# Attention and pair products in one kernel: six of eight key steps on kept score pieces instead of five

## The reference, cut to what matters

```
# layer 0: attention over the 4096 positions of one image
xf   = gn(x)                                   # (4, 256, 4096)
f, g = Wq xf + bq,  Wk xf + bk                 # 32 channels each
h    = Wv xf + bv                              # 256 channels
s    = einsum('bki,bkj->bij', f, g)            # 4096 x 4096 scores per image
beta = softmax(s, axis=1)                      # over i
x    = x + gamma * einsum('bci,bij->bcj', h, beta)
# layer 1: products of all channel pairs
y    = relu(bn(w1 gn(x) + b1))                 # 32 channels
packed = y[rows] * y[cols]                     # 528 pairs
x    = x + relu(bn(w2 packed + b2))
```

## Time and profile before

| what | value |
|---|---|
| median of three runs | 2107.17 us |
| profiled execution, its own time | 2109.38 us |
| its span (first to last instruction) | 2107.6 us |
| TensorE matmuls busy | 2056.0 us (98%) |
| VectorE busy | 1656.5 us (79%) |
| ScalarE busy | 1539.2 us (73%) |
| GpSimd busy | 1479.8 us (70%) |
| DMA queue q1, share of 16 engines | 66.6% |
| chain that ended last, share of TensorE | 86% |

### The profile page before, as it was taken

One profiled execution on the slowest core, in us unless ns is written; L12 is line 12 of the kernel. 1 busy time (PEld: TensorE's weight loads), 2 busy tenths in 40 slices (PEclk: granted clock), 3 DMA queues, 4 the chain that ended last, 5 costly groups with the idle time before them and its releaser, 6 DMA issues.

```text
span 2107.6 us, 48084 instructions
## 1 busy us (share of the span) xinstructions
PE 2056.0 (98%) x17334; PEld 1611.1 (76%) x17334; DVE 1656.5 (79%) x3617; ACT 1539.2 (73%) x2456; POOL 1479.8 (70%) x2110
## 2 busy tenths in 40 slices
PE   5899999999999999999999999999999999999999
PEld 3688888888877777777877777777787777777854
DVE  8788988778777877878768788777877768777767
ACT  5677777767776777778777787777777777777767
POOL 3265666667677777878768787777867767677766
PEclk9999999999999999999999999999999999999999
DMA  5165778776476788778478678887836767675632
GB/s 190 37 101 103 129 143 143 139 132 113 84 133 122 146 158 150 154 145 156 98 140 140 117 156 142 159 167 139 157 78 134 144 124 140 118 142 94 139 72 81
DMA packets 728269, 271.89 MB, mean 129 GB/s; under 512 B 674240, under 2 KB 681152, under 8 KB 728000
## 3 DMA queue, kind: packets, MB, share of 16 engines
q1 hardware_dynamic: 728032, 268.82, 66.6%
HBM read 77.07 MB, written 19.92 MB: 46 GB/s over the span
## 4 chain that ended last, share of the span: by engine, by line
PE 86%; DVE 5%; POOL 3%; ACT 2%; issue 2%; DMA 1%; SPq 0%; DVEq 0%; ACTq 0%; POOLq 0%
PE acc L1784 19%; PE acc L1772 19%; PE acc L1773 18%; PE tps L1577 5%; PE acc L1577 5%; PE sps L1597 4%; PE acc L1571 3%; PE tps L1648 3%; PE tps L1650 2%; PE acc L1648 1%; POOL kb L1162 1%; PE tps L1612 1%; DVE ks L863 1%; PE tps L1634 1%; POOL xl L1139 1%
## 5 line engine op out<-in xcount | busy, mean ns | idle before, releaser
L1162 POOL TENSOR_TENSOR kb<-ks,kb 128x512 f16<-128x512 f32 x630 | 760.3, 1211 | 412.1 <-DVE kb L891 315.6
L1772 PE MATMUL acc<-hth,kt 128*128 128x257 f16 x2520 | 587.2, 273 | 1.1 <-DMA kt<-kb 1.1
L1773 PE MATMUL acc<-htl,kt 128*128 128x256 f16 x2520 | 586.6, 273 | 0.0
L1333 ACT ACTIVATE ph<-sps,esc 128x512 f16<-128x512 f32 x394 | 269.5, 684 | 339.7 <-PE sps L1597 329.8
L1345 ACT ACTIVATE ks<-ks,kbias,esc 128x512 f32<-128x512 f32 x630 | 498.9, 805 | 0.0
L1784 PE MATMUL acc<-hth,kt 128*128 128x257 f16 x2520 | 385.8, 274 | 0.0
L863 DVE TENSOR_SCALAR_CACHE_REDUCE ks<-acc 128x512 f32<-128x512 f32 x378 | 259.2, 686 | 158.8 <-PE acc L1577 157.0
L1772 PE MATMUL acc<-hth,ph 128*128 128x257 f16 x1576 | 367.3, 274 | 0.0
L1773 PE MATMUL acc<-htl,ph 128*128 128x256 f16 x1576 | 366.9, 273 | 0.0
L1784 PEld LDWEIGHTS acc<-hth,kt 128*128 128x128 f16 x2520 | 247.7, 98 | 100.6
L1772 PEld LDWEIGHTS acc<-hth,kt 128*128 128x128 f16 x2520 | 247.0, 98 | 41.6 <-issue 6.2
(11 more groups left out here) (254 smaller groups left out, 3444.7 us busy)
## 6 DMA issues: line engine op xcount, KB each, us to landing
rt<-turned SPq DMA_DIRECT2D x96, 256.0 KB, 4.9
xt<-x SPq DMA_DIRECT2D x46, 512.0 KB, 4.5
xb<-x SPq DMA_DIRECT2D x32, 512.0 KB, 4.7
out<-zt SPq DMA_DIRECT2D x45, 256.0 KB, 2.7
kt<-kb SPq DMA_TRANSPOSE x630, 3.2
yb<-turned SPq DMA_DIRECT2D x36, 128.0 KB, 2.6
rt<-turned SPq DMA_DIRECT2D x72, 64.0 KB, 2.2
turned<-yb SPq DMA_DIRECT2D x12, 256.0 KB, 2.5
```

The source lines that it names most:

```text
L1162: tt(kb[:, m % KB_RING, 1], ks[:, m % KS_RING], kb[:, m % KB_RING, 0], ALU.subtract).then_inc(kl_ok, 1)
L1333: A(ph[:, v % SLOTS], sps[v % 2][:], ACT.Exp, scale=esc[:]).then_inc(ph_ok, 1)
L1772: mm(bank[:, 0:C + 1], high[:, q], hth[:, c * QT + q], start=(s8 == 0 and q == 0), stop=False)
L1773: mm(bank[:, 0:C], high[:, q], htl[:, c * QT + q], start=False, stop=False)
```

## The change

`KEPT_STEPS` grows from five to six (1, 2, 3, 5, 6, 7), so steps 0 and 4 alone are made. The sixth kept number (r = 5) has its low half made by VectorE right after its cast (`LOW_BY_DVE`), counted by a semaphore of its own, `kd_ok`; GpSimd keeps five low halves per tile. ScalarE makes three high halves per tile in place of two, VectorE still makes three casts. The tables of steps are set anew, and the rings `ks`, `kb` and `kt` get one slot more each. For that memory the ring of x falls from 14 to 13 chunks. So one chunk more per image passes through `xt`, and `VORD` and `V_EARLY` are changed.

```
-KEPT_STEPS = (1, 2, 4, 6, 7)
+KEPT_STEPS = (1, 2, 3, 5, 6, 7)
-HIGH_BY_ACT = (0, 2)
-EXP_AT = (3, 4, 6, 7, 8)
-CAST_AT = (None, 3, None, 6, 7)
-LOW_AT = (2, 3, 5, 7, 8)
-TURN_AT = (3, 4, 6, 8, 9)
+HIGH_BY_ACT = (0, 2, 4)
+EXP_AT = (1, 2, 4, 5, 6, 8)
+CAST_AT = (None, 1, None, 4, None, 7)
+LOW_AT = (0, 2, 3, 5, 6, None)
+TURN_AT = (2, 3, 5, 6, 7, 9)
+LOW_BY_DVE = (5,)
-ROW_AT = 6
+ROW_AT = 5
-KS_RING = 8
-KB_RING = 4
-KT_RING = 5
+KS_RING = 9
+KB_RING = 5
+KT_RING = 6
-XR = 14
+XR = 13
...
-        VORD = (4, 0, 5, 1, 6, 2, 3, 7)
+        VORD = (4, 0, 5, 3, 6, 1, 2, 7)
...
-        V_EARLY = (12, 15, 18, 21)
+        V_EARLY = (11, 15, 19, 26)
 
         def in_place(b, c):
-            return b == 0 or (c < XR - NCH if b == 1 else c < 4)
+            return b == 0 or (c < XR - NCH if b == 1 else c < 3)
...
+        def low_done(m):
+
+            own = m % KEPT in LOW_BY_DVE
+            return (kd_ok if own else kl_ok), sum((k % KEPT in LOW_BY_DVE) == own for k in range(m + 1))
...
             def turn(tile, r):
 
                 m = count_of(tile, r)
-                sp.wait_ge(kl_ok, m + 1)
+                sp.wait_ge(*low_done(m))
...
                     if m >= KS_RING:
-                        dve.wait_ge(kl_ok, m - KS_RING + 1)
+                        dve.wait_ge(*low_done(m - KS_RING))
...
                 V.tensor_copy(kb[:, m % KB_RING, 0], ks[:, m % KS_RING]).then_inc(kc_ok, 1)
+                if r in LOW_BY_DVE:
+                    dve.wait_ge(kc_ok, casts_until(m))
+                    V.tensor_tensor(kb[:, m % KB_RING, 1], ks[:, m % KS_RING], kb[:, m % KB_RING, 0],
+                                    ALU.subtract).then_inc(kd_ok, 1)
...
-                        if b < LASTB and J == NCH - 1 and t in (13, 16, 19, 22):
-                            normed(("v", b + 1, VORD[(13, 16, 19, 22).index(t)]))
+                        if b < LASTB and J == NCH - 1 and t - 1 in V_EARLY:
+                            normed(("v", b + 1, VORD[V_EARLY.index(t - 1)]))
...
                         for r in range(KEPT):
-                            if t % NCH == LOW_AT[r] % NCH and is_kept_tile(tile - LOW_AT[r] // NCH):
+                            if LOW_AT[r] is not None and t % NCH == LOW_AT[r] % NCH and is_kept_tile(tile - LOW_AT[r] // NCH):
                                 kept_low(tile - LOW_AT[r] // NCH, r)
```

More of the change, by code:

```diff
@@ L200, in build @@
         kbias_ok = sem("kbias_ok")
-        kp_ok, kc_ok, kl_ok = sem("kp_ok"), sem("kc_ok"), sem("kl_ok")
+        kp_ok, kc_ok, kl_ok, kd_ok = sem("kp_ok"), sem("kc_ok"), sem("kl_ok"), sem("kd_ok")
         kt_in = [sem(f"kt_in{i}") for i in range(KT_RING)]
@@ L1225, in _ @@
                             low(("qk", b + 1, 2 * (J - 3) + 1))
-                        if t in (14, 17, 20, 23) and b < LASTB and J == NCH - 1:
-                            low(("v", b + 1, VORD[(14, 17, 20, 23).index(t)]))
+                        if t - 2 in V_EARLY and b < LASTB and J == NCH - 1:
+                            low(("v", b + 1, VORD[V_EARLY.index(t - 2)]))
                         if t == 20 and b and 1 <= n < SHARED - 1:
@@ L1456, in attend @@
                             high(("qk", b + 1, 2 * (J - 2)))
-                        if b < LASTB and J == NCH - 1 and t in (12, 15, 18, 21):
-                            high(("v", b + 1, VORD[(12, 15, 18, 21).index(t)]))
+                        if b < LASTB and J == NCH - 1 and t in V_EARLY:
+                            high(("v", b + 1, VORD[V_EARLY.index(t)]))
             act.wait_ge(set_dve, mark["scaled_qkv"])
```

## The result

The changed kernel takes 2145.06 us in the median of four runs (2143.75 to 2146.36), the kernel before 2106.99 in the same comparison: 1.018 times, 95% interval 1.0162 to 1.0197. That is 38 us slower, where 18 us faster was forecast, and it lies outside the forecast range of 2078 to 2106.

A forecast was written before the change was run, and what follows sets the result against it. The prediction took TensorE's rate of columns as the bound. Its terms, -28 + 2 + 4 + 2 + 2 = -18 us, took 2107.2 to 2089 us, with 8 in 10 odds of 2078 to 2106.

The forecast's parts named there:

- What bounds the kernel, what is removed: TensorE's matmuls, busy 98%, bound the kernel; 126 tiles each lose one made step of 0.22 us, 28 us less.
- DMA and the ring kb: 126 more transposing copies, each issued six steps or more before TensorE reads it; bounds 0 and +10, taken +2.
- `kt` is free in time: The slot of a copy issued at step 9 was last read in step 7, the others one step or more ahead.
- The third rival: Copies come late at a DMA share of 0.95, L1772 waits on `kt`; 0.5 us per tile makes 2137; chance 0.09.
- ScalarE: Changed exponentials add 35 us in all, covered by 340 us idle ahead of L1333 except in the first kept tile.
- VectorE: New subtraction at 0.97 us, net +46 us of work, mostly covered by waits for pieces; bounds 0 and +37, taken +4.
- The burst of step 7: VectorE work of 4.0 us in a step of 1.55, in 24 chunks of outputs, some 0.2 us each.
- the VectorE rival: VectorE takes a good part back, piece banks run out in most tiles: 13 to 21 us, 2098 to 2106; chance 0.13.
- the prediction's own signs: L1577 waits far over 5 us more mean the VectorE rival; L1772 waits over 10 us, landing median over 4, late copies.
- The ring of x: Image 0, J = 5: a load behind the added query use makes VectorE wait 2 to 3 us; bounds 0 and +6, taken +2.
- First kept tile: At 88 to 108 us two more ScalarE exponentials before tile 2 are not covered; bounds 0 and +3, taken +2.
- its four terms: Costs set against the -28 us: first kept tile +2, VectorE +4, DMA +2, ring of x +2.

The follow-up runs named there:

- the run with a copy too many: Kernel before, five kept steps, with the fifth pair of halves turned twice per tile, first into an unread spare place: 2123.56 us, +15.1.
- The three list entries: Changed kernel with `product_low` at t = 10 and 11, `qk_high` at t = 23, statistics at (5, 20) and (6, 2); with a sixth kb slot 2110.61 us, +3.9.
- the two other runs with `z_out` ahead: Changed kernel with `z_out` at t = 3: 2149.71 us; with sixth kb slot, moved entries and `z_out` at t = 4 ahead of the kept halves: +20.9.

## Why the prediction was wrong, point by point

**What bounds the kernel, what is removed.** Right: 504 matmuls went, and a chunk without disturbance is 0.88 us shorter. "TensorE has almost no wait to give back" was right too. What the prediction priced too low is the reverse, the waits that it can gain.

**DMA and the ring kb: this step failed.** The prediction took +2, with a cover of "six steps or more" from the issue of a copy until TensorE reads `kt`. That cover held: TensorE waits 1.6 us there. But a landing also frees a kb slot, and that has its own, shorter deadline, 6, 6 and 5 steps by the tables. Against it stood the same landings that the prediction quoted, up to 9.9 us. That term was missing from the sum. In its place the runs show a wait of ScalarE for landings of 140 us, and a sixth kb slot was worth 20 us by itself. "`kt` is free in time" failed as well: the queue waited 300 us for TensorE (79 before), and a seventh slot was worth 12 us. The load was right: 75.6 - 66.6% in the run with a copy too many is 199 us of 16 engines, 1.58 us a copy, where the prediction had at most 1.74. Taking the copies out was worth 22 us. The third rival named the right resource, and the bursts of `rt` loads too, but the wrong place: it watched L1772.

**ScalarE.** The prediction took the 340 us in which ScalarE idles for scores as cover. The added work (+35 us forecast, 1581 - 1539 = 42 measured) leaves 154 us of idle time ahead of the same instruction. But idle time is no cover for an instruction that stands in line and waits, with `z_out`, the division and `qk_high` behind it. The earlier trace rows had the sign: L1343 already waited 15.3 us for landings, and the prediction gave it no price. It isn't the added high half that waits most: 102 of the 140 us fall to the two that ScalarE made before too.

**VectorE: the place was right, the size was not.** The new subtraction took 873 ns against 970. The burst of step 7 was forecast to cost +4 with the rest; the product taken out of it gave 9 us, and the wait that went was two steps on, at t = 9, as the prediction has it. The three list entries together were worth 19 us without the sixth slot and 14 with it. By the prediction's own signs this was the VectorE rival: the waits of L1577 for VectorE (L1587 now) were to grow by 5 us and grew from 4.5 to 32.2. The gap at 1290 us shows that such a wait can begin with a landing, so this sign doesn't part the rivals.

**The ring of x.** Forecast +2, measured +5.0, and at the other neighbour: the prediction looked at the next use behind the added one. The use ahead counts, since the chunk must land before its own use, and the load waits its turn in the queue.

**First kept tile.** Forecast +2: image 0, J = 0 is 0.76 us longer, although two of its four tiles save 0.22 us each, so it cost 1.2 us.

**The sum** erred because its four terms were each bounded alone. Even the upper bounds of all four (+3, +37, +10, +6) would have reached 2135 and not 2145: the kb slot had no term, and the lower clock after TensorE's new gaps (5 us) none.

**The rule of the Trainium skill** (SBUF — State Buffer, section "SBUF: two separate sides") for a VectorE instruction with two SBUF inputs and a GpSimd instruction that reads SBUF is that the later one waits for the whole of the other. The trace agrees: the new subtraction L900 takes 693 ns in the median and 1780 at most. The rule also bears on an instruction that the prediction left as it was: L956, two inputs in SBUF, went from a mean of 968 to 1182 ns, though nothing in it was changed, with its median at 1258 in place of 685.

## What to carry to other kernels

A wait has two prices: what the waiting instruction delays by itself, and what stands behind it in its engine's list. Before adding an instruction that waits for a ring slot, work out each deadline of the landing (the reader's and the slot's next writer's) and read what follows the writer in its list; an engine's idle share is no cover for that. When terms go through the same list, bound them together.

## What was not expected of the hardware

One VectorE instruction can last through several GpSimd operations. One product with both inputs in SBUF took 3.99 us (685 ns is the median of before) beside four GpSimd operations that followed each other without a gap from 969.56 to 974.92 us. The longest took 3.98 and 3.99 us in the two other runs with `z_out` ahead too, and 3.87 us with the sixth low half on GpSimd. In the kernel before the longest was 1754 ns. That it lost its turn several times fits these times; no row shows the turns themselves.

Gaps of 2.6 to 3.1 us on TensorE were followed by 3.4 us at a granted clock of 0.51, three times in the changed kernel. Not every such gap was: in the run with the ring of x alone TensorE idled 2.92 us ahead of 379.85 us, and the clock stayed at 1.00. What decides it, these runs don't show.
